# Cross-attention and mixture FFN on one core: another order of weight and activation slots in SBUF, two tiles loaded during the last value products, and the late value loads of the first batch issued behind its context loads

## The reference

```python
def _L0_xattn_ref(query, key):
    a = jnp.einsum('bqd,bkd->bqk', query, key)
    e = jax.nn.softmax(a, axis=-1)
    c = jnp.einsum('bqk,bkd->bqd', e, key)
    return c
...
base_out = jnp.einsum('bsi,oi->bso', x, base_w) + base_b
res_hidden = jnp.einsum('bsi,ri->bsr', x, A)
logits = jnp.einsum('bsi,ei->bse', x, router_w)
...
x = x + _L0_xattn_ref(_layernorm(x, axis=-1), ctx_4096)
x = x + _L0_ffn_ref(_layernorm(x, axis=-1), L0_ffn_base_w, L0_ffn_base_b, L0_ffn_A, L0_ffn_B, L0_ffn_router_w)
```

## Time and profile before

| what | before |
|---|---|
| device time, median of 3 runs (range) | 1458.26 us (1456.08 to 1459.49) |
| the profiled execution: its own time, its span | 1453.22 us, 1451.5 us |
| busy in the span: PE, PE weight load, DVE, ACT, POOL | 94%, 76%, 65%, 44%, 22% |
| mean granted TensorE clock | 0.985 of full speed |
| `ctx_high` on ACT, `ctx_low` on DVE, one piece | 1,450 ns, 1,718 ns |
| `weight_high` on ACT, `weight_low` on DVE, one pair | 1,054 ns, 1,249 ns |
| `tile_high` on ACT, `tile_low` on DVE, one piece of four | 621 ns, 826 ns |
| `value_high` on ACT, `value_low` on DVE, one block | 626 ns, 683 ns |
| eight transposes of `x2T_last` on PE at full clock, start to the next product | 0.70 us |
| a transposed group's high part on ACT, low part on DVE | 914 ns, 1,090 ns |

### The profile page before, as it was taken

The page is one execution under the profiler, slowest core; times in us unless marked ns, Lnnn a source line. Parts: engine busy times, 40 slices in busy tenths (PEclk is TensorE's granted clock), DMA queues, the critical chain, the costliest instruction groups (busy, mean ns, idle before and its releaser), DMA issues.

```text
span 1451.5 us, 18409 instructions
## 1 busy us (share of the span) xinstructions
PE 1365.1 (94%) x6777; PEld 1107.6 (76%) x6777; DVE 950.6 (65%) x1199; ACT 634.3 (44%) x797; POOL 325.4 (22%) x247
## 2 busy tenths in 40 slices
PE   5899999999999999999799988899989999999998
PEld 4678787787878787787688766677767788888886
DVE  6486777777687767768355467676767746445553
ACT  3355554545564554545311266677767501100100
POOL 2002002020201102020414724444445011111110
PEclk9899999999999999999999999999999999999999
DMA  9958678687867768679656698999996987887874
GB/s 323 271 179 261 198 255 252 202 249 235 276 213 250 231 223 253 211 251 178 198 166 173 185 280 268 264 313 293 302 308 166 359 250 240 254 256 240 257 246 130
DMA packets 216840, 350.59 MB, mean 242 GB/s; under 512 B 26992, under 2 KB 129392, under 8 KB 207088
## 3 DMA queue, kind: packets, MB, share of 16 engines
q1 hardware_dynamic: 198192, 282.31, 64.5%
q0 software_dynamic: 10528, 52.85, 11.7%
q10 hardware_dynamic: 8064, 14.68, 2.9%
HBM read 266.11 MB, written 99.41 MB: 252 GB/s over the span
## 4 chain that ended last, share of the span: by engine, by line
PE 35%; DMA 13%; DVE 3%; issue 2%; ACT 1%; SPq 1%; POOL 0%; POOLq 0%; ACTq 0%; DVEq 0%
PE scores L829 11%; PE scores L830 10%; PE scores L831 10%; DMA res<-x_scratch 7%; DMA y_scratch<-y_out,yrow_i 3%; DMA w_in<-in_wT_dram 2%; PE work L865 1%; PE work L866 1%; DMA a_in<-xT_scratch 1%; DVE w_l L1382 1%; DVE raw_l L1148 1%; ACT y_out L1054 1%; ACT b_hl L1046 0%; DMA hs_scratch<-hg,pos_i 0%; DVE x L1184 0%
## 5 line engine op out<-in xcount | busy, mean ns | idle before, releaser
L829 PE MATMUL scores<-w_h,a_h 128*128 128x512 f32 x896 | 354.5, 396 | 14.0 <-DVE a_l L1389 8.1
L831 PE MATMUL scores<-w_h,a_l 128*128 128x512 f32 x896 | 352.4, 393 | 0.0
L830 PE MATMUL scores<-w_l,a_h 128*128 128x512 f32 x896 | 352.4, 393 | 0.0
L1030 ACT ACTIVATE a_h<-a_in 128x512 fp32r<-128x512 f32 x168 | 94.3, 621 | 317.5 <-DMA a_in<-xT_scratch 210.5
L1389 DVE TENSOR_TENSOR a_l<-a_in,a_h 128x512 fp32r<-128x512 f32 x168 | 130.7, 826 | 127.2 <-ACT a_h L1030 123.1
L829 PEld LDWEIGHTS scores<-w_h,a_h 128*128 128x128 f32 x896 | 169.7, 189 | 53.6 <-issue 15.2
L831 PEld LDWEIGHTS scores<-w_h,a_l 128*128 128x128 f32 x896 | 169.5, 189 | 38.3
L830 PEld LDWEIGHTS scores<-w_l,a_h 128*128 128x128 f32 x896 | 169.7, 189 | 37.1
L695 PE MATMUL scores<-ctxT_h,nT_h 128*112 128x494 f32 (+1 forms) x512 | 174.9, 342 | 10.6 <-DVE ctxT_l L1138 6.2
L1148 DVE TENSOR_TENSOR raw_l<-raw_in,val_h 128x512 fp32r<-128x512 f32 x192 | 155.0, 826 | 44.8 <-ACT val_h L959 44.6
L1557 POOL TENSOR_TENSOR res<-res,bias_b 128x512 f32<-128x512 f32 x56 | 86.4, 1543 | 407.9 <-DMA res<-x_scratch 388.0
(11 more groups left out here) (149 smaller groups left out, 1977.8 us busy)
## 6 DMA issues: line engine op xcount, KB each, us to landing
ctxT_in<-in_ctxT_dram SPq DMA_DIRECT2D x64, 750.0 KB, 7.6
a_in<-xT_scratch SPq DMA_DIRECT2D x42, 1024.0 KB, 8.7
raw_in<-in_ctx_dram SPq DMA_DIRECT2D x32, 1280.0 KB
w_in<-in_wT_dram SPq DMA_DIRECT2D x32, 512.0 KB, 9.6
x<-in_x_dram SPq DMA_DIRECT2D x8, 1792.0 KB, 9.3
xT_scratch<-xT_st SPq DMA_DIRECT2D x8, 1792.0 KB, 11.8
res<-x_scratch SPq DMA_DIRECT2D x56, 256.0 KB, 7.7
y_add<-y_scratch SPq DMA_DIRECT2D x56, 256.0 KB, 5.3
```

What stands on the lines that cost most here:

```text
L829: pe.matmul(o, ah, wh, start=(k == 0), stop=False)
L830: pe.matmul(o, ah, wl, start=False, stop=False)
L831: last = pe.matmul(o, al, wh, start=False, stop=(k == KD - 1))
```

## The change

Three things change.

1. In SBUF `w_h` moves behind the first two activation slots. Slot 0 now lies over the last context buffer, `ctxT_h` and the start of `prob`; slot 1 over the rest of `prob` and `raw` chunk 0; `w_h` over `raw` chunks 1 to 3. Slot 2 stays.
2. In the last batch the load of tile 0 is issued ahead of the `hs_scratch` fill and the `xT_scratch` store, and tile 1's takes the place that tile 0's had. ACT and DVE do tile 0 at e = 9 to 12, weight pairs 0 to 4 at e = 15 to 22, and pairs 5, 6 and 7 behind the last value block, with tile 1 behind them. Tile 2 is done whole ahead of the four transposes, and in DVE `finish(0)` stands ahead of both.
3. In batch 0 value chunks 2 and 3 are asked for behind context pieces 6 and 7, no longer behind 4 and 5.

```diff
-FIRST_W_AT = (8, 10, 12, 14, 16, 18, 20, 22)
-FIRST_A_AT = 23
+FIRST_W_AT = (15, 17, 19, 21, 22)
+FIRST_A_AT = (9, 10, 11, 12)
...
         w_l, w_in = sb_in("w", [P, WR, WP, BANK], stack)
-        w_h = sb("w_h", [P, WR, WP, BANK], F32R)
...
         for i in range(AR):
+            if i == AR - 1:
+                w_h = sb("w_h", [P, WR, WP, BANK], F32R)
...
                     load_ctxT(b, j)
-                    if first and j - LR + 2 < CH:
-                        load_raw(0, j - LR + 2)
+                    if first and j - LR in (2, 3):
+                        load_raw(0, j - LR)
...
                     for j in range(PAIRS // 2, PAIRS):
                         load_w(j)
+                    sp.wait_ge(xT_stored, (NB - 2) * 16)
+                    load_a(0)
                     sp.wait_ge(fresh_ready, 2)
...
-                    sp.wait_ge(val_used, b * (CH * NT) + 2 * NT)
-                    sp.wait_ge(xT_stored, (NB - 2) * 16)
-                    load_a(0)
+                    sp.wait_ge(val_used, b * (CH * NT) + NT)
+                    load_a(1)
...
             sp.wait_ge(val_used, NB * CH * NT)
-            load_a(1)
...
-                        if j == 5:
-                            act.wait_ge(val_used, b * (CH * NT) + NT)
+                        if j == 0:
+                            act.wait_ge(val_used, b * (CH * NT) + 2 * NT)
+                        if j == 3:
+                            act.wait_ge(val_used, b * (CH * NT) + 3 * NT)
                         weight_high(j)
-                    if stage == "last" and e == FIRST_A_AT:
-                        act.wait_ge(val_used, b * (CH * NT) + 3 * NT)
-                        tile_high(0, range(KD // AQ))
+                    if stage == "last" and e in FIRST_A_AT:
+                        tile_high(0, (FIRST_A_AT.index(e),))
...
                 if g == 0:
+                    for j in range(len(FIRST_W_AT), PAIRS):
+                        if j == 6:
+                            act.wait_ge(val_used, NB * CH * NT)
+                        weight_high(j)
+                    tile_high(1, range(KD // AQ))
                     for n in range(CH):
                         normalise_last(n)
-                    act.wait_ge(val_used, NB * CH * NT)
-                    tile_high(1, range(KD // AQ))
                     continue
                 if g == 1:
+                    tile_high(2, range(KD // AQ))
                     for n in range(NX):
                         x2T_last(n)
...
                 if g == 0:
+                    weight_low(5)
                     last_stats()
+                    weight_low(6)
                     shift(mv2, rs2, nb2, rstd2, bias2, NB - 1)
+                    weight_low(7)
                     tile_low(1, range(KD // AQ))
                     continue
+                finish(g - 1)
                 if g == 1:
+                    tile_low(2, range(KD // AQ))
                     for n in range(NX):
                         x2T_last(n)
-                finish(g - 1)
```

More of the change, by code:

```diff
@@ L1097, in _ @@
                 if g < PAIRED:
-                    tile_high(g + 1, range(KD // AQ) if g in ROUTING else (0, 1))
+                    if g > 1:
+                        tile_high(g + 1, range(KD // AQ) if g in ROUTING else (0, 1))
                     store_tile(g - 1)
@@ L1119, in _ @@
                         expert_high(s + 2)
-                if g < PAIRED and g not in ROUTING:
+                if 1 < g < PAIRED and g not in ROUTING:
                     tile_high(g + 1, (2, 3))
@@ L1362, in one @@
                         weight_low(FIRST_W_AT.index(e))
-                    if not new and e == FIRST_A_AT:
-                        tile_low(0, range(KD // AQ))
+                    if not new and e in FIRST_A_AT:
+                        tile_low(0, (FIRST_A_AT.index(e),))
                     if new and e - 3 in QT_AT:
@@ L1495, in _ @@
                     hidden_back("tail", NB)
-                if g < PAIRED:
+                if 1 < g < PAIRED:
                     tile_low(g + 1, range(KD // AQ) if g in ROUTING else (0, 1))
-                elif i + 1 < TT:
+                elif g >= PAIRED and i + 1 < TT:
                     tile_low(visit_of(g) + 1, (0, 1) if c == EARLY else (2, 3))
```

## The result

The changed kernel took 1450.35 us (median of 6 runs, 1447.12 to 1453.99), the kernel before, beside it on the same chip, 1458.86 (6 runs, 1456.08 to 1461.41): a ratio of 0.9944, 95% interval 0.9921 to 0.9966. The forecast was 1443.4. The direction held; of 14.9 us, 8.5 came (8.2 by the ratio), and the time is just outside the range of 1438.5 to 1449.5.

The account below looks back on a forecast made before the run. PE, busy 94% of the span, was taken as the bound, its waits as what can be won. Batch 0's 5.4 us plus the linear start's 9.5 gave 14.9, so 1458.26 - 14.9 = 1443.4 us, range 1438.5 to 1449.5.

Parts of the forecast that it names:

- Batch 0, 5.4 us forecast: In batch 0, moving value chunks 2 and 3 back ends PE's wait for context piece 6: gain 5.4 us.
- the two terms: Batch 0: PE's 3.7 us wait for context piece 6, and 1.7 us of low clock behind it.
- `x2` lands at 72.0 now: Batch 0's residual load stays behind the same bytes, so lateness costs nothing to 1 us; taken as nothing.
- The bound of 2.1 us: Batch 0: at the slowest load rate context piece 7 lands at 47.7, a stall of 2.1 us; costed at nothing.
- the 0.7 us of cover counted for piece 6: Batch 0: context piece 6 is ready at 44.9 and PE needs it at 45.6.
- The linear start, 9.5 us forecast: Between attention and linear layer, tile 2's start moves from 717.52 to 708.0: gain 9.5 us, bounds 7.9 to 11.1.
- pairs 5 to 7 are in time: Linear start: weight pairs 5 to 7 are ready before PE needs them, covered by 2.6 us at the tightest.
- its new wait: Third transpose within tile 1: PE newly stalls 1.3 to 2.5 us behind tile 2's work; taken as 1.9.
- Cover 1.3 us, cost nothing: Batch 7's value products: after tile 0's load, block 10 is ready at 658.5, PE needs it at 659.78; no cost.
- The 3.5 us that I had read for the load itself: Tile 0's load, queued behind weight pair 7, takes 3.5 us and lands at 656.4.
- The lead is absorbed: Rival: expert tiles, 860 to 1060 us, swallow most of the 9.5 us, giving 1450 to 1455; chance 0.09.
- batch 0 gives little: Rival: piece 7 or `x2` late and clock low leave 0.6 us in batch 0; total 10.1, 1448.2; chance 0.14.

Follow-up runs that it names:

- b2: The kernel before once more, unchanged, for a further profiled execution: 1459.89 us (ratio 1.0005).
- s0: The kernel before with gathers of expert matrices cut to 8 of 64 rows from the ninth slot on: 1426.99 us (ratio 0.9792).
- e1: The changed kernel with part 3 undone (value chunks 2 and 3 again behind context pieces 4 and 5): 1452.35 us (ratio 0.9953).
- e2: The kernel before with part 3 alone (value chunks 2 and 3 behind context pieces 6 and 7): 1460.84 us (ratio 1.0001).
- e4: The changed kernel once more, unchanged: 1452.91 us (ratio 0.9948).
- s1: The changed kernel with gathers of expert matrices cut to 8 of 64 rows from the ninth slot on: 1420.42 us.
- r1: The changed kernel with tile 0's load asked for behind the `hs_scratch` fill: 1468.51 us (ratio 1.0084).
- n2: The changed kernel with tile 0's load asked for ahead of weight pairs 4 to 7: 1447.18 us (ratio 0.9925).
- e3: The changed kernel with batch 0's `x2` load asked for right behind the next batch's `xn`: 1450.58 us (ratio 0.994).
- e5: The changed kernel with batch 0's `x2` load right behind `xn`, value chunk 2 behind context piece 5 and chunk 3 behind piece 7: 1450.40 us (ratio 0.9935).
- s3: The changed kernel with batch 0's `x2` load right behind `xn` and gathers cut to 8 of 64 rows from the ninth slot on: 1419.62 us.
- d0: The changed kernel with batch 0's `x2` load right behind `xn`, once more, as zero of the delay series: 1449.93 us.
- n1: The changed kernel with tile 0's load ahead of weight pairs 4 to 7 and batch 0's `x2` load right behind `xn`: 1446.45 us (ratio 0.9918).
- w0: The kernel before with 75 transposes of the identity on PE ahead of its first work: 1462.49 us (ratio 1.0024).
- w1: The changed kernel with 75 transposes of the identity on PE ahead of its first work: 1452.14 us (ratio 0.9959).
- `x2` edit: Batch 0's `x2` load asked for right behind the next batch's `xn`, ahead of that batch's context pieces 0 to 2; on the changed kernel 1450.58 us.
- w3: The changed kernel with batch 0's `x2` load right behind `xn` and 75 transposes on PE ahead of its first work: 1449.92 us (ratio 0.9938).
- d12: The changed kernel with batch 0's `x2` load right behind `xn` and 74 transposes on PE ahead of batch 0's first scores: 1455.64 us.
- d24: The changed kernel with batch 0's `x2` load right behind `xn` and 166 transposes on PE ahead of batch 0's first scores: 1464.91 us.

## Why the prediction was wrong, point by point

The marks of the executions, in us (those with transposes at the start are left out of the first table):

| executions | batch 1 starts | mean |
|---|---|---|
| old order of chunks (before, b2, s0, e1) | 140.0, 138.0, 136.1, 137.5 | 137.9 |
| new order (after, e2, e4, s1, r1, n2) | 141.1, 140.1, 139.1, 138.8, 139.0, 135.4 | 138.9 |
| new order, `x2` early (e3, e5, s3, d0, n1) | 133.5, 134.2, 135.5, 135.8, 136.2 | 135.0 |

| linear start, batch 7 to tile 2 | range | mean |
|---|---|---|
| as before (before, b2, w0, s0, e2) | 95.8 to 96.9 | 96.4 |
| changed, tile 0's load behind the weights (12) | 87.5 to 91.1 | 88.9 |

**Batch 0, 5.4 us forecast: nothing came.** This is the step that failed, in two places. "Gain of this part: 3.7 + 1.7 = 5.4 us, bounds 3.3 and 5.4": the two terms were read rightly, from an execution in which they are larger than in the others. With `x2` early, batch 1 starts 2.9 us ahead of the old order on the mean, and not 5.4. (Its 135.0 is about where the forecast had it, 140.0 - 5.4 = 134.6; what was unusual is the 140.0.) So the lower bound had to be near zero.

The second place is "`x2` lands at 72.0 now, behind the same bytes as before, and DVE takes it up at 77.4 ... Nothing to 1 us": it lands at 77.6. The bytes are the same, but I counted them as if the DMA engines stayed busy. They stand half idle for 8 us, which by the shares is 4.5 us of full work left undone, and the bytes moved past this hole make everything behind them later. In the five executions with the old order DVE never waits for `x2`; in all seven with the new order and no edit of `x2` (w1 among them) it waits 2.1 to 5.1 us, and the load lands at 74.4 to 77.7 (mean 76.5), where it lands at 71.1 to 73.9 (mean 72.8) with the old order. The new order alone timed 1.0001.

On its other points the step was right: no execution with the new order has a wait for a context piece. Piece 7 landed at 47.3 with PE through piece 5 at the same time, so it costs nothing. (The bound of 2.1 us for it was too wide: the 0.7 us of cover counted for piece 6 hold for piece 7 too.)

**The linear start, 9.5 us forecast: 7.4 on the mean of the traces, 6.9 to 7.6 timed (e1).** In the profiled execution it is 8.9 to 9.0. From tile 0's first product on, the forecast holds: from there to the finish of tile 2 it takes 52.4 us on the mean with the old linear start and 42.7 with the new one, which is 9.7 less. There is no wait ahead of tile 1, pairs 5 to 7 are in time, and the third transpose has its new wait (0.7 to 1.7 us, forecast 1.3 to 2.5, taken 1.9).

Mis-sized is what lies ahead, "Cover 1.3 us, cost nothing" for tile 0's load. Its first product stands 44.0 us behind batch 7's first row maximum in all five executions with the old start, 45.1 to 48.2 (mean 46.2) in the twelve with the new one, and 43.5 in n1 and n2, where the load goes ahead of the weights. So the term that was put at nothing cost 2.2 us on the mean, and 1.1 in the profiled execution. PE's waits for `raw_l` in batch 7's value products are 1.6 to 3.5 us, 1.4 before. Part of the reason is in DVE's queue behind the first piece:

```profile
658.46 0.69 DVE L1396 TENSOR_TENSOR a_l<-a_in,a_h 128x512 fp32r<-128x512 f32 x1 [1.55 <-ACT a_h L1032]
...
659.32 1.41 DVE L1191 SCALAR_TENSOR_TENSOR x<-scores,rinv,x 112x512 f32<-112x512 f32 x2
660.64 0.68 DVE L1155 TENSOR_TENSOR raw_l<-raw_in,val_h 128x512 fp32r<-128x512 f32 x1
```

The piece's own low part and a residual stand ahead of block 10's low part. The forecast counted 2.1 us from the landing until block 10 is ready; here it is 3.6, so no cover was left. This is read from one trace, and no run tests the residual's place.

The other part is the landing. Counted from batch 7's first row maximum, it was forecast at 18.9 us; it is 19.1 in the profiled execution (657.7) and 19.1 to 21.7 in the twelve, 20.2 on the mean. The 3.5 us that I had read for the load itself are right: from weight pair 7 to it there are 3.4 to 3.6 us in nine of the twelve and 4.6 to 5.2 in three. It is the pair that lands later, by 0.2 to 1.7 us. The Trainium skill's 6.15 us for 1 MB (DMA: Bandwidth & Descriptors, Bandwidth, "Measured", for loads that GpSimd issues) would put the landing at 659.1, which is 21.6 us behind batch 7's start; the mean of 20.2 lies about halfway between the two, and for the distance behind the pair the row is the better one.

**"The lead is absorbed".** In the one pair of traces it looks so: 7.8 us of lead at tile 2, 0.8 behind at the end. From the finish of tile 2 to the last tile it took 712.3 us in the profiled execution before, but 721.0, 721.1 and 724.7 in three others with the old linear start (b2, w0, e2), and 720.1 on the mean of thirteen with the new one (714.1 to 725.0). The odd one is again the execution that I had predicted from: alone the tiles 12 to 28 took 307.1 us there, and 316.1 to 317.5 in the three others. It was 5.0 us faster than its median, as I had noted, without asking where. The delays pass through with a slope near 1, so that a lead is not lost behind tile 2.

**The sum.** Nothing from batch 0 and 7.4 us give 1458.3 - 7.4 = 1450.9; measured 1450.35. (That they agree within 0.6 us is luck, given the spread of the runs.) The forecast's chance of 0.14 for "batch 0 gives little" named the right part and the right load, and its 10.1 us still took the linear start too high, and left 0.6 us to batch 0. The spread between executions is wide (1448.4 to 1466.9 for 35 runs of the kernel before), which is why single traces mislead here.

**What stays open.** The `x2` edit is worth 3.9 us on the means of the table, and 5.7, 2.8, 3.3 and -0.9 us in the four pairs of traces that differ by it alone (e4 and e3, w1 and w3, s1 and s3, n2 and n1); the same pairs timed give 2.3, 2.2, 0.8 and 0.7. A mean of 2.7 against 1.5 is within the spread of single executions, but the timed gain may be truly smaller. How often `x2`'s wait is small by itself, as in n2, in runs without a profile can't be seen. That the length of the half-rate start sets the size of the stall at piece 6 rests on executions as they came, since the edit meant to set it did not.

## What to carry to other kernels

A stall at a load early in a kernel depends on how early the engine gets there; before a gain is read from it, compare several executions, above all if the profiled one is some microseconds off its median. When a transfer is moved later in a queue, ask what the DMA engines do in the place it leaves: if nothing can take it, every later load moves back by the work left undone there. When a piece of work is moved between others, count all that stands ahead of them in every engine's queue, and not only the piece itself. And price a delay by a known one: 166 idle transposes in front showed that a shift of 15 us reaches the end, which no reading of the busy stages could.

## What the runs showed of the hardware

- PE's first score matmuls ran at half rate (0.61 us for 494 columns, later 0.39) until 23.5 to 25.2 us in 10 of the 15 executions without extra transposes, and until 21.7 and 22.2 in two (n2, r1). In the three others (the profiled kernel before, e3, e5) they ran at the full rate from the first, at 18.6 to 19.5. PE had worked since 14 to 15 us in all of them, with one gap of 1.1. The profile's row shows a granted clock of 1.00 in these stretches all the same; only the counts and durations tell. The Trainium skill says that the clock starts low and that the point at which it rises differs between runs of one kernel (TensorE: Matmul & The Clock Gate, What's actually happening). The traces agree: it lies at 18.6 us or earlier in one execution and at 25.2 in another.
- Transposes alone brought the full rate too (from 0.21 to 0.11 us apart, at 4.6 us in w0, 20.1 in d12 and 18.7 in d24). But 75 of them ahead of the first work didn't keep it: after 2.4 and 3.2 us without work the rows show 0.50 for some 6 to 8 us (w1, w0).
- Where POOL's gathers and scatters fill the DMA engines, the seven 512 KB weight loads of chunk 1 take very different times from issue to landing for the same code. Issues of the profiled kernel before from 845 to 890 us, and of the changed one from 835 to 880 (KB each, median us to landing):

```profile
w_in<-in_wT_dram SPq DMA_DIRECT2D x7, 512.0 KB, 7.4
```
```profile
w_in<-in_wT_dram SPq DMA_DIRECT2D x7, 512.0 KB, 25.3
```

It is not the change: the changed kernel again had 9.5 us (e4), the kernel before again 19.0 (b2, eight loads). A DMA engine takes turns between the queues that have work for it, says the Trainium skill (DMA: Bandwidth & Descriptors, Queues, rings and completion order). The trace shows both queues at work there, and no run here shows how the turns fall.
